# Behind the scan: the silu of keys and queries split between ScalarE's tanh and VectorE's product, and the keys' squares amid the routing's gates

## The reference, cut to what matters

```python
x = x + 0.5 * ffn(layernorm(x))          # router: 8 experts, top 2
x = x + attn(layernorm(x))
x = x + 0.5 * ffn(layernorm(x))

# attn, 8 heads of 32:
q = silu(x @ Wq); k = silu(x @ Wk); v = silu(x @ Wv)
log_f = log_sigmoid(x @ Wf1 @ Wf2)
beta = sigmoid(x @ Wbeta) * 2
k = k / sqrt(sum(k * k, per head) + 1e-6)
# scan over time per head: S = exp(log_f) S + a (b.S) + k v^T, with a, b from -beta k and k, twice per token
o = q . S                                 # then gate, per-head RMS norm, Wo

# ffn, per token: probs = softmax(x @ router_w.T); the two largest weigh two experts
```

## Time and profile before

| | us |
|---|---|
| median of three runs | 1864.21 |
| lowest, highest | 1859.53, 1866.02 |
| the profiled execution | 1851.54 |
| its span, first to last instruction | 1849.6 |
| TensorE busy (share of the span) | 1583.3 (86%) |
| VectorE busy | 1113.3 (60%) |
| ScalarE busy | 786.7 (43%) |
| GpSimd busy | 767.4 (41%) |

### The profile page before, as it was taken

One profiled execution on the slowest core, in us unless ns is written; L12 is line 12 of the kernel. 1 busy time (PEld: TensorE's weight loads), 2 busy tenths in 40 slices (PEclk: granted clock), 3 DMA queues, 4 the chain that ended last, 5 costly groups with the idle time before them and its releaser, 6 DMA issues. The chain is left out here.

```text
span 1849.6 us, 68392 instructions
## 1 busy us (share of the span) xinstructions
PE 1583.3 (86%) x26476; PEld 1286.8 (70%) x26477; DVE 1113.3 (60%) x3370; ACT 786.7 (43%) x1829; POOL 767.4 (41%) x986
## 2 busy tenths in 40 slices
PE   5499999999577978878887888977886999999994
PEld 4499999999435565455654556535564999999994
DVE  7646444443457886787868878588773556444441
ACT  2143333333266444673447734476332443333331
POOL 2554522222145552646527466183651235422222
PEclk9999999999788999798998889978997999999997
DMA  9563432322300200002000020000102833332324
GB/s 301 174 201 70 93 48 46 51 46 48 78 3 8 68 26 23 4 7 70 23 23 5 9 67 23 23 5 7 46 23 94 253 78 75 74 64 46 51 46 114
DMA packets 84239, 116.28 MB, mean 63 GB/s; under 512 B 12952, under 2 KB 74464, under 8 KB 82016
## 3 DMA queue, kind: packets, MB, share of 16 engines
q1 hardware_dynamic: 56160, 74.17, 13.2%
q0 software_dynamic: 27360, 37.80, 11.7%
q10 hardware_dynamic: 608, 2.96, 0.5%
HBM read 64.87 MB, written 54.21 MB: 64 GB/s over the span
## 5 line engine op out<-in xcount | busy, mean ns | idle before, releaser
L1069 POOL DMA_INDIRECT x<-ffn_yout,ffn_place x142 | 222.0, 1563 | 532.5 <-DVE ffn_yout L1001 455.3
L1007 DVE TENSOR_TENSOR ffn_inner<-ffn_inner,ffn_bank 128x512 f32<-128x512 f32 x142 | 97.5, 687 | 343.1 <-PE ffn_bank L877 338.5
L958 ACT ACTIVATE ffn_inner<-ffn_bank 128x512 f32<-128x512 f32 x142 | 84.8, 597 | 458.9 <-PE ffn_bank L877 458.9
L877 PE MATMUL ffn_bank<-ffn_tileT,ffn_gate_now 128*128 128x128 f32 x2272 | 280.0, 277 | 0.0
L877 PE MATMUL ffn_bank<-ffn_tileT,ffn_up_now 128*128 128x128 f32 x2272 | 277.5, 275 | 0.0
L887 PE MATMUL ffn_bank<-ffn_w,ffn_inner 128*128 x1136 | 268.9, 380 | 1.8 <-DVE ffn_yout L1001 1.8
L877 PEld LDWEIGHTS ffn_bank<-ffn_tileT,ffn_gate_now 128*128 128x128 f32 x2272 | 268.2, 194 | 0.1
L877 PEld LDWEIGHTS ffn_bank<-ffn_tileT,ffn_up_now 128*128 128x128 f32 x2272 | 265.8, 192 | 0.0
L887 PEld LDWEIGHTS ffn_bank<-ffn_w,ffn_inner 128*128 128x128 f32 x1136 | 205.0, 191 | 24.5 <-issue 2.5
L820 ACT COPY ffn_gate_now<-ffn_w 128x1024 f32 x142 | 148.4, 1045 | 29.4 <-issue 21.9
L820 DVE COPY ffn_up_now<-ffn_w 128x1024 f32 x142 | 99.4, 700 | 59.5 <-issue 47.8
(11 more groups left out here) (614 smaller groups left out, 3141.4 us busy)
## 6 DMA issues: line engine op xcount, KB each, us to landing
ffn_w<-in_w1t_dram SPq DMA_DIRECT2D x16, 1024.0 KB, 5.4
ffn_tile<-xs SPq DMA_DIRECT2D x122, 130.0 KB, 2.1
ffn_w<-in_w2t_dram SPq DMA_DIRECT2D x16, 512.0 KB, 6.7
at_a_sb<-x SPq DMA_DIRECT2D x32, 256.0 KB, 2.8
ffn_x<-in_x_dram SPq DMA_DIRECT2D x16, 256.0 KB, 5.0
x<-ffn_x SPq DMA_DIRECT2D x16, 256.0 KB, 6.4
x<-at_a_sb SPq DMA_DIRECT2D x16, 256.0 KB, 2.1
xs<-ffn_empty SPq DMA_DIRECT2D x23, 130.0 KB, 3.0
```

The source lines that it names most:

```text
L877: t = pe.matmul(bank[:, i * P:(i + 1) * P], half_now[half][b][:, k, i * P:(i + 1) * P], rowsT[b][:, k * P:(k + 1) * P], start=(k == 0), st ...
L958: act.activation(inner[b][:, :], p_g[b][:, :], ACT.Silu).then_inc(s_silu, 1)
L1007: dve.tensor_tensor(inner[b][:, :], inner[b][:, :], p_u[b][:, :], ALU.mult).then_inc(s_act, 1)
L1069: pool.indirect_dma_start(total, bass.IndirectOffsetOnAxis(ap=place[b][:, 0:1], axis=0), yout[b][:, :], None, compute_op=ALU.add).then_inc ...
```

## The change

In `turnover`:

- Silu of a job becomes two steps: ScalarE writes tanh of half the product to the tile (L1426's place, new semaphore s_th), and VectorE multiplies 1 + tanh by the product, which it reads from PSUM (`gated`). For keys the result is twice the silu, and the norm absorbs the 2 with eps4 (four times epsilon) in place of epsk. For queries the weights wq are halved once in the attention's setup (two VectorE instructions in `setup_vector_end`, semaphore s_half), so the product is already halved there. `between` takes Silu with scale 2 for queries.
- Tanh is now taken from "exp_and_others". There are three table loads per turnover instead of two: one behind the deviation's root, one amid the gates, one behind the logarithms.
- ScalarE: job 0's tanh goes ahead of the gates' copies, job 1's behind the second copy, beta's tanh and jobs 2 and 3 behind the fourth, with a load of the set with Ln. The logarithm of sum 0 goes ahead of the routing's exponential, the other three behind it. Then come a load, factor 0, root 0, the tanhs of jobs 4 to 7, root 1, sums and factor of the first chains, roots 2 and 3.
- TensorE: squares 0 and 1 go behind job 4 amid the gates, square 2 ahead of job 5, square 3 behind it, beta's products 0 and 1 ahead of job 7, the counts behind job 7.
- VectorE: the products of jobs 0 to 3 and beta's addition go ahead of the logits. Behind the ranks come scaled key 0, beta times key 0, job 4's product, decays 0 and 1, job 5's product, key 1, the products of jobs 6 and 7, differences 0, the slots, keys 2 and 3, decay 2, differences 1, and the first key product.
- GpSimd waits for the jobs of queries one by one instead of all eight.

The diff, cut to its core:

```diff
-    JOB_BANKS = (0, 1, 5, 6, 7, 2, 3, 0)
+    JOB_BANKS = (0, 1, 5, 6, 7, 5, 2, 3)
-    SQUARES = [psum[i] for i in (1, 5, 6, 7)]
-    BETAS = [psum[i] for i in (2, 3, 6, 5)]
+    SQUARES = [psum[i] for i in (0, 1, 6, 0)]
+    BETAS = [psum[i] for i in (1, 6, 6, 4)]
...
                     if i == GT // 2:
                         pe.wait_ge(s_lf, 4)
                         job(4)
+                        square(0)
+                        square(1)
...
                 r.gate_tensor(pe, 0, spare=amid)
+                square(2)
+                pe.wait_ge(s_ev, 3)
                 job(5)
+                square(3)
                 job(6)
-                pe.wait_ge(s_ev, 1)
+                pe.wait_ge(s_beta, 1)
+                beta(0)
+                beta(1)
                 job(7)
                 r.count_tensor(pe, 0)
-                square(0)
-                square(1)
-                pe.wait_ge(s_beta, 1)
-                beta(0)
-                square(2)
-                beta(1)
-                square(3)
                 beta(2)
                 beta(3)
...
-                    act.activation(both(t, g, c), psum[JOB_BANKS[j]][:, :], ACT.Silu).then_inc(s_ev, 1)
+                    act.activation(both(t, g, c), psum[JOB_BANKS[j]][:, :], ACT.Tanh, scale=0.5 if j < 4 else 1.0).then_inc(s_th, 1)
...
+                def amid(i):
+                    if i == 1:
+                        job(1)
+                    if i == GT // 2 - 1:
+                        act.activation(fg[2 * RANK:FG, :], fg[2 * RANK:FG, :], ACT.Tanh, scale=0.5).then_inc(s_bt, 1)
+                        job(2)
+                        job(3)
+                        act.preload_act_table_set("natural_log_exp_and_others")
...
                 r.std_scalar(act, 0)
-                r.turn_scalar(act, 0)
+                act.preload_act_table_set("exp_and_others")
+                job(0)
+                r.turn_scalar(act, 0, spare=amid)
+                ln_norm(0)
                 r.choose_scalar(act, 0)
+                for j in range(1, 4):
+                    ln_norm(j)
+                act.preload_act_table_set("exp_and_others")
                 keyed.open_scalar(act)
                 act.wait_ge(s_lf, 4)
+                keyed.factor(act, 0)
+                norm_root(0)
+                for j in range(4, 8):
+                    job(j)
+                norm_root(1)
+                keyed.sums(act, 0)
+                keyed.factor(act, 1)
+                keyed.sums(act, 1)
+                norm_root(2)
+                norm_root(3)
...
+                def gated(j):
+                    t, w, g, c = JOBS[j]
+                    dve.wait_ge(s_th, j + 1)
+                    dve.scalar_tensor_tensor(out=both(t, g, c), in0=both(t, g, c), scalar=1.0, in1=psum[JOB_BANKS[j]][:, :],
+                                             op0=ALU.add, op1=ALU.mult).then_inc(s_ev, 1)
...
                 r.norm_vector(dve, 0, xr)
+                gated(0)
+                gated(1)
+                dve.wait_ge(s_bt, 1)
+                dve.tensor_scalar(fg[2 * RANK:FG, :], fg[2 * RANK:FG, :], 1.0, None, ALU.add).then_inc(s_beta, 1)
+                gated(2)
+                gated(3)
                 r.logits_vector(dve, 0)
                 r.share_vector(dve, 0)
                 r.rank_vector(dve, 0)
...
+                normal(0)
+                late_key(0)
+                gated(4)
+                dve.wait_ge(s_n1, 4)
                 keyed.decay(dve, 0)
+                dve.wait_ge(s_kb, 1)
+                keyed.decay(dve, 1)
+                gated(5)
+                normal(1)
+                late_key(1)
+                gated(6)
+                gated(7)
+                keyed.differences(dve, 0)
+                r.slot_vector(dve, 0)
+                normal(2)
+                normal(3)
+                late_key(2)
+                late_key(3)
+                keyed.decay(dve, 2)
                 keyed.differences(dve, 1)
```

More of the change, by code:

```diff
@@ L1112 @@
     s_w: object
+    s_half: object
     loads: int
@@ L1152, in attn @@
         ta = last("ta", [P, UN, CHAINS, SUB + CT])
-        for n in ("w", "const", "init", "stat", "in0", "in1"):
+        for n in ("w", "const", "init", "stat", "half", "in0", "in1"):
             kept.append(ctx.enter_context(nc.semaphore(f"at_{n}")))
-        s_w, s_const, s_init, s_stat, *s_x = kept
+        s_w, s_const, s_init, s_stat, s_half, *s_x = kept
         NT = BATCH * PT // P
@@ L1208, in setup_vector_end @@
             for c in range(KCH):
+                i = dve.tensor_scalar(wq[:, c, :], wq[:, c, :], 0.5, None, ALU.mult)
+            i.then_inc(s_half, 1)
+            for c in range(KCH):
                 dve.tensor_scalar(wo[:, c, :], wo[:, c, :], nw[:, c:c + 1], None, ALU.mult)
             Routing.start(dve, table, lasting)
-        setup = Setup(setup_sync, setup_scalar, setup_vector, setup_vector_end, s_const, s_w, loads)
+        setup = Setup(setup_sync, setup_scalar, setup_vector, setup_vector_end, s_const, s_w, s_half, loads)
         env = locals()
@@ L1451, in _ @@
                 r.std_scalar(act, 0)
-                r.turn_scalar(act, 0)
+                act.preload_act_table_set("exp_and_others")
+                job(0)
+                r.turn_scalar(act, 0, spare=amid)
+                ln_norm(0)
                 r.choose_scalar(act, 0)
[L1454 to L1457, removed]
-                act.preload_act_table_set("natural_log_exp_and_others")
+                for j in range(1, 4):
+                    ln_norm(j)
+                act.preload_act_table_set("exp_and_others")
                 keyed.open_scalar(act)
                 act.wait_ge(s_lf, 4)
-                for j in range(4):
-                    act.wait_ge(s_ss, j + 1)
-                    act.activation(rn[j][:, :], SQUARES[j][:, :], ACT.Ln, bias=epsk[:, 0:1]).then_inc(s_n1, 1)
-                    act.wait_ge(s_n1, j + 1)
-                    act.activation(rn[j][:, :], rn[j][:, :], ACT.Exp, scale=-0.5).then_inc(s_n2, 1)
-                    if j < 2:
-                        keyed.factor(act, j)
-                        keyed.sums(act, j)
-                act.wait_ge(s_kb, 2)
+                keyed.factor(act, 0)
[8 more added lines that the diff above has]
+                norm_root(3)
+                act.wait_ge(s_ev, 8)
                 act.wait_ge(s_st, 16 * BATCH)
@@ L1610, in job @@
                         pe.wait_ge(s_ev, BANK_FREE[j])
+                    if j == 4 and setup is not None:
+                        pe.wait_ge(setup.s_half, 1)
                     if j == 6 and routes:
@@ L1687, in job @@
                     act.wait_ge(s_mm, j + 1)
-                    act.activation(both(t, g, c), psum[JOB_BANKS[j]][:, :], ACT.Silu).then_inc(s_ev, 1)
+                    act.activation(both(t, g, c), psum[JOB_BANKS[j]][:, :], ACT.Silu, scale=1.0 if j < 4 else 2.0).then_inc(s_ev, 1)
                 def turn(i):
```

49 lines of the change are left out of this document (27 added, 22 removed).

## The result

The changed kernel took 1880.37 us (median of 4 runs, 1876.52 to 1881.43) against 1863.39 for the kernel before (4 runs), a ratio of 1.0093 with a 95% interval of 1.0074 to 1.0112: 17.0 us slower, where 12.7 were forecast. The profiled execution took 1880.78 us, its span is 1879.0, 29.4 above that of before.

A forecast was written before the change was run, and what follows sets the result against it. VectorE's unbroken 20.8 us from logits to first key product was taken to set each turnover's exit. 1.96 + 1.27 - 1.50 + 2.5 = 4.2 us later, three times +12.7, gave 1877 us; 8-in-10 range 1866 to 1883.

The forecast's parts named there:

- rival 4: Amid the gates: TensorE drops to half pace in one or more turnovers, 3.4 more, 1880 us; chance 0.74 together with the forecast.
- Squares amid the gates: TensorE's squares 0 and 1 behind job 4 (1.72), with copies 0.24 late, start the logits 1.96 us later per turnover.
- Root's wait: Behind the ranks, VectorE waits 1.27 us per turnover for ScalarE's root ahead of the first normalization; bounds 0 to 3.8.
- Queries' products: Between logits and first key product, four new VectorE products for q add 2.5 us per turnover; bounds 2.4 and 2.7.
- Addition gone: Beta's addition leaves VectorE's work between logits and first key product, saving 1.50 us per turnover with its gap.
- Contention: VectorE's later normalizations may or may not meet GpSimd's wide product: -1.0 to +1.0 us, taken as 0.
- GpSimd's start: GpSimd's products, behind first scaled key and q product, start near 986.8 against 987.78, 1.0 us earlier.
- Rival 2: GpSimd's products set the exit and start 3.0 us earlier in each of three turnovers: faster, 1855 us; chance 0.09.
- rival 1: The chains' loop swallows VectorE's lateness: 3.7 of 4.2 us vanish per turnover, no change, 1866 us; chance 0.14.
- rival 3: Each table switch holds ScalarE beyond its load by a 1.3 us drain: 3.7 more per turnover, 1888 us; chance 0.03.

The follow-up runs named there:

- run 1: Changed kernel without VectorE's four products of the queries' silu, queries left as bare tanh; ratio 1.0051 to the kernel before.
- run 7: Kernel before, with beta's 1 added inside the late keys' product and the separate addition (L1505) left out; ratio 0.9990 to the kernel before.
- Run 8: Kernel before with beta's 1 folded as in run 7, plus picks, notes and places moved into the chains' loop's waits; ratio 1.0015 to the kernel before.
- run 10: Kernel before with two more GpSimd products, results unused, ahead of its first chain in each turnover; ratio 1.0035 to the kernel before.
- run 2: Changed kernel with two more GpSimd products, results unused, ahead of its first chain in each turnover; ratio 1.0067 to the kernel before.
- run 4: Changed kernel with the routing's slot arithmetic moved from behind the first differences to directly behind the ranks; ratio 1.0061 to the kernel before.
- run 3: Changed kernel with squares 0 and 1 behind the router's products instead of amid the gates, first logarithm behind the choice; ratio 1.0101 to the kernel before.
- 5: Changed kernel reordered: squares behind gates, decays 0 and 1 in the gates' wait, beta's 1 folded, loads, slots and banks moved; ratio 1.0019 to the kernel before.
- 6: As 5, with slots, picks, notes and places moved into the chains' loop's waits, two copies of the counts added; ratio 1.0020 to the kernel before.
- run 9: As 5, with beta's second product ahead of job 6 on TensorE, the third and fourth in other banks; ratio 1.0002 to the kernel before.
- run 11: As run 9, with GpSimd's first chain held back by a wait until VectorE's second late key; ratio 1.0002 to the kernel before.

## Why the prediction was right, and where its terms were not

Direction and range were right, and so was the mechanism: the logits late, the stretch longer, and what VectorE has in the stretch comes out at the exit (run 1). The size is in part luck. The turnovers themselves cost 23.5 us (10.5, 12.0 and 1.0 of the table), nearly twice the 12.7; 4.4 came back in stretches that the sum does not have. That the time is nearly the 1880 of rival 4 is luck too, since that rival has the half clock and not the contention. Point by point:

- *Squares amid the gates, +1.96.* Right once the clock is taken out; as they stand the three differences are 1.94, 3.62 and 4.95. Take from each start-to-logits time what the half clock cost in it, which is (1 - granted clock) times the length of the window, for two windows: up to 8 us ahead of the logits, and those 8. (Third turnover after: 0.92 over 32.44 us and 0.72 over 8 make 2.6 and 2.2, and 40.44 becomes 35.6.) What is left is 33.7 to 33.9 in all twelve turnovers of the four kernels with the old ScalarE and TensorE order (before, 7, 8, 10), and 35.6 to 35.8 in all twelve of the four with squares amid the gates (after, 1, 2, 4). With ScalarE's work there and no squares (3, 5, 6, 9, 11) it is 33.9 to 34.0 in 13 of 15 turnovers, 33.2 and 35.3 in the others. So the squares are 1.7 and ScalarE's lateness 0.2, the two parts of the 1.96. The 35.3 is the third turnover of run 3, where ScalarE set the gates: there its work alone costs 1.5, and the squares on top of it only 0.3, as the forecast's 975.1 against 975.38 had it.
- *Root's wait, +1.27.* 1.43. The forecast's own durations give less: 981.5 and 3.0 of ScalarE's work are 984.5, which is 1.0 behind the rank. *Queries' products, +2.5.* They are there at 0.67 to 0.68 each, 2.4 with overlap. *Addition gone, -1.50.* Gone from the stretch. But run 7 shows what it was worth in the kernel before: 0.06. The step took an unbroken row of work on VectorE to mean that nothing else was close behind. In the sum it does no harm, since the forecast also priced the root's wait and the two nearly cancel (+1.43 - 1.50); that they are one and the same slack is argued, not shown.
- *Contention, -1.0 to +1.0, taken as 0.* This is the term that was mis-sized. The normalizations went from 3.67 to 4.63 in sum (0.69, 1.50 and 2.44 now), the two slot operations from 0.74 to 1.67: +1.9 per turnover, outside the bounds. Those looked at normalizations alone; that the slots were moved from ahead of GpSimd's chains to beside them (before, they ended at 985.19 and the chains began at 987.78) was not seen. Run 2 moves GpSimd's work and gets 1.4 of it back, run 4 moves the slots and gets 1.6 back (1.3 on the slots, 0.3 on the last normalizations).
- *Half pace.* Rival 4 was more than a rival: TensorE was at half clock amid the gates in all three turnovers. Reckoned as above it cost 11.7 us from start to logits over three turnovers, and 6.7 in the trace before. But it is not fixed to the order: the runs 1, 2 and 4 with the same gates lost 10.3, 8.4 and 8.1 (in run 4's third turnover job 4 took 1.96), the runs 7, 8 and 10 on the old order 6.4, 5.0 and 8.0. By the means of these, an estimate, about half of the 5.0 belongs to the change and half to this pair of traces.
- *GpSimd's start.* 8.84 behind the logits, forecast 8.6 (978.2 to 986.8); before it was 11.52. But "1.0 earlier" did not come: from the turnover's start it was 47.01 before and is 47.95, since the half clock made the logits 1.7 later than forecast. The gaps for factors came ahead of the fourth and fifth chain as forecast. Rival 2 falls with runs 2 and 10.
- *Rivals 1 and 3.* Run 1 excludes the first. The third would need idle time around the three loads of a turnover; in the nine loads of the trace the next operation begins 0.01 to 0.02 behind the load.
- *Not priced:* the time between last key product and next start, where nothing was changed, gave 3.5 back. In the second and third of these TensorE was granted 0.95 and 0.94 instead of 0.91 and 0.93; that the one explains the other is argued, not shown.

Sum: 12.0 (stretches) + 10.5 (starts) + 1.0 - 0.9 - 3.5 = 19.1 in the traces, 17.0 in the medians. Against the 12.7: the stretches are 5.2 over their part of the forecast (contention, 1.9 each, less 0.5 in all that no row places), the starts 4.6 over theirs (clock 5.0 in this trace, the squares 0.4 under), the turnovers' loops 1.0; and 4.4 came back.

Can the change pay? With its order rebuilt (9, 11) it stands level with the kernel before, within 0.2%. Its earlier roots take ScalarE's chain out of VectorE's way (no wait for a root is left in run 9's stretches), and the queries' products put 2.4 us back onto the one engine that sets the exit. No version was found that beats the kernel before by more than the measurement is uncertain; 0.9990 (0.9976 to 1.0004) for the folded 1 is the nearest.

## What to carry to other kernels

When VectorE work is moved past the moment at which GpSimd starts, price each moved instruction with two SBUF operands at what is left of the GpSimd instruction that it may meet, plus its own time, tiny ones too: here 0.17 became 0.68. An unbroken row on one engine does not say that it alone is critical; before counting a removed instruction as a gain, look at what the next two on it are waiting for. And waits in a loop shared with GpSimd are not free room for small operations.

## What the runs showed of the hardware

- A VectorE operation of two SBUF operands does not run beside a GpSimd product but behind it: it ended 0.56 (after, 1003.98), 0.55 (run 10, 1008.72) and, for the small one, 0.08 us (after, 1010.15) behind the end of the GpSimd instruction that was running as it began. It goes both ways: GpSimd's pair L2104 took 2.00 beside two normalizations, 1.55 elsewhere. Run 8 shows it for a copy with one SBUF input too: L302 began at 1020.44, amid GpSimd's product of 1019.70 to 1021.26, and took 0.85 instead of 0.17. The Trainium skill says this in "SBUF — State Buffer", SBUF: two separate sides: the pair of ports that the two engines share is an exclusive lock, whoever starts first has it for the whole instruction, and a VectorE operation needs it when it has two SBUF inputs, or runs in a mode that uses both ports. The rows just given agree for two inputs; whether the copy ran in such a mode no run shows. By that rule the forecast would have had to count five such operations behind GpSimd's start instead of three.
- More work on GpSimd made one kernel's stretch shorter (run 2, -1.4) and the other's longer (run 10, +0.5). The rows of both runs show why: a shift of 2 us on an engine that has room re-deals which instructions meet.
- TensorE's half clock can sit on job 4 (3.34 and 3.76 instead of 1.96), or behind the gates (run 11, four squares 6.2 instead of 3.8), in nearly the same program; by these rows each such place is worth 1.4 to 2.4 us, as much as a part of the change.
